# A fused DLRM tower on Trainium2: two weight loads and a gather wait change places in SyncE's program

## Chip, cores, metric

One core of one Trainium2 chip. The metric is the device time of one execution in microseconds. The kernel before has a median of 537.44 us over three runs (534.53 to 537.46).

## The reference, cut to what matters

A batch of 512 samples looks up one row of 1024 numbers in each of eight tables. Two of the eight fields pass a two-layer "not" net (Wn1 with relu, Wn2 with tanh). Then pairs of fields are fused by "and" nets (Wa1, Wa2) and one "or" net (Wo1, Wo2), the results and the unprocessed fields are averaged, and three top layers follow. Everything is float32.

```python
x_not = jnp.take(field_vectors, not_idx, axis=1)
t = jnp.tanh(jax.nn.relu(x_not @ Wn1 + bn1) @ Wn2 + bn2)
iv = field_vectors.at[:, not_idx, :].set(t)
...
and_out = pair_fuse(and_pairs, Wa1, ba1, Wa2, ba2)
or_out = pair_fuse(or_pairs, Wo1, bo1, Wo2, bo2)
...
z = sum_res / count
h = jnp.maximum(jnp.concatenate([z, dense_ctx], axis=1) @ W_top1 + b_top1, 0.0)
h = jnp.maximum(h @ W_top2 + b_top2, 0.0)
y = h @ W_top3
```

## The kernel before

**Layout.** XR holds float32 activations in eight buffers, features on the partitions, batch along the free axis. WR holds seven slots of raw weights, 128 x 1024 float32 (512 KB) each, called pieces; piece n covers two output tiles of one quadrant of a weight matrix. Each piece is split for TensorE into a high and a low part: ScalarE copies WR to WO with rounding (split_w, L631), VectorE subtracts (L846) and raises w_lo. Activations are split in the same way into XO (L718 and L852 for the first field; L660 and L924 later). A product group is the twelve matmuls of 128 x 512 of one output tile (four k tiles, times high x high, high x low, low x high; L1117); each raises the semaphore quarter by one. Two groups use one piece.

**The big layers.** The matrices Wn1, Wn2 and Wa1 are multiplied by a scheme of seven products over 2 x 2 blocks, which needs sums of activation blocks (operand_sum, L986) and of weight quadrants. For Wn1 ("stage 0") the products come in the order P1, P2, Q5, Q6, Q7, P4, Q3. P1 uses the quadrant B11 (pieces 0 and 1, in WR slots 0 and 1) on the first "not" field, P2 the quadrant below it (pieces 2 and 3, in slots 4 and 5) on the same field. Q5 needs B11 + B12: once P1 has been fed, the two pieces of B12 are loaded into slots 2 and 3 (L465) and VectorE adds them to slots 0 and 1 (L866, raising t1_sum). ScalarE later copies these sums to slots 2 and 3 (L782), where GpSimd's accumulating DMA (add_quadrant, L526) adds a third quadrant for Q6.

**The start.** GpSimd gathers the rows of the first not field in four indirect DMAs (L496, semaphores x0_in[0..3]) and of the second in four more (L500, x1_in[0..3]). TensorE transposes them, in between the first product groups (L1144 for the first field, L1193 for the second), ScalarE copies the transposed banks out to XR (x0_keep at L724, raising x0_raw; x1_keep at L729, raising x1_raw), and P1's groups run on half the batch at a time, as rows come in.

**Who decides the order.** Each engine has its own program, written out by hand, and works it in order; between engines there are only semaphores. SyncE issues nearly all weight loads: load(n) (L448) puts piece n in its slot and raises raw_in of that slot. At the start it issues load(0) and load(1), then waits for x0_in[1] and issues load(2), waits for x1_in[3] (L460) and issues load(3), P2's second piece. Then come the two loads of B12, each behind a wait for x0_raw, 5 for the first and 6 for the second (x0_done(1, h) is 5 + h: the third and fourth of the four copies at L724 that stand in a row there). Then load(8) and all others follow, behind waits on quarter and w_lo.

**Readers near the change.** VectorE's program has, in this order: the four low parts of the first field's second half (L852), the two L866 (each waits for its raw_in), split_w(2), whose w_lo = 3 P2's first group waits for, and split_w(3), whose w_lo = 4 P2's third group waits for. ScalarE splits piece 2 (L631), copies the second field's banks (L729), evacuates P1 (L689), splits piece 3 (L631), makes the two copies L782, and copies the last two banks of the second field (L729), which P2's third and fourth groups need freed. TensorE transposes the second field's second half before P2's first group and again between its first and second (turn_second_field(1, ...), L1193).

Of the kernel before, what the change touches and what calls it, by code (L numbers as in the profile page):

```python
# [22 lines left out]
BT = B // P  # L23
# [111 lines left out]
def raw_slot(n):  # L135
    if n >= 2 * OZ:
        return (n - 2 * OZ) % 7
    if n in R_PIECES:
        return R_SLOT + R_PIECES.index(n) % 3
    s, half = stage_of(n // 2), half_of(n // 2)  # L140
    if s == 0 and product_of(n // 2) in (Q6, P4):
        return 2 + n % 2
    return 2 * (half if s == 2 else s) + n % 2
# [15 lines left out]
def x_done(e, kk):  # L159

    return x0_done(1, 2 * e + kk) if e < 2 else 8 + 2 * (e - 2 - sum(e >= i for i in KEPT_X)) + kk + 1


def x0_done(h, pair):


    return 4 * h + pair + 1
# [63 lines left out]
def dlrm_tower(nc, table, ints, weights, cols, consts, identity, dense_t, w_dense, out, zero_row):  # L231
    table_quarters = table.rearrange("v (q c) -> (v q) c", q=Q)

    with ExitStack() as ctx:
# [3 lines left out]
        def sem(name):  # L238
            return ctx.enter_context(nc.semaphore(name))
# [80 lines left out]
        x1_in = [sem(f"x1_in{b}") for b in range(BT)]  # L320
# [97 lines left out]
        def block_rows(n):  # L418

            e, h = n // 2, n % 2  # L420
            if e < OZ:
                kh, mh = LOADED[product_of(e)]
                return 8 * matrix_of(e) + 4 * mh + 2 * h, k_half(e, kh)
            if 2 * n < FIRST[Z]:
                i = n - 2 * OZ
                return 8 * (4 + i // 8) + 2 * (i % 4), i // 4 % 2
            i = n - FIRST[Z] // 2
            if 2 * n < FIRST[TOP]:
                matrix, kh, mh = Z_PARTS[i // 2]
                return 8 * matrix + 4 * mh + 2 * (i % 2), kh  # L430
            return 8 * KT + 2 * (i % 2), i // 2 - len(Z_PARTS)

        def quadrant_rows(block, kh):
            return weights[block:block + 2, :, 512 * kh:512 * (kh + 1)].rearrange("m p c -> p m c")

        def raw_piece(slot):
            return WR[:, slot, :].rearrange("p (m c) -> p m c", m=2)
# [4 lines left out]
        @block.sync  # L442
        def _(sp):
            sp.dma_start(int_in, ints).then_inc(ints_in, 16)

            def load(n):
                slot = raw_slot(n)
                sp.dma_start(raw_piece(slot), quadrant_rows(*block_rows(n))).then_inc(raw_in[slot], 16)  # L448

            def load_after(n, split):  # L450

                sp.wait_ge(w_lo, split + 1)
                load(n)

            load(0)
            load(1)

            sp.wait_ge(x0_in[1], 16)
            load(2)
            sp.wait_ge(x1_in[BT - 1], 16)  # L460
            load(3)

            for h in range(2):
                sp.wait_ge(x0_raw, x0_done(1, h))
                sp.dma_start(raw_piece(2 + h), quadrant_rows(4 + 2 * h, 0)).then_inc(raw_in[2 + h], 16)  # L465
            sp.wait_ge(quarter, 4)
            load(8)
            for n, split in ((9, 2), (12, 3), (13, 8), (16, 9), (14, 10), (15, 11), (17, 12), (20, 13), (28, 14),
# [4 lines left out]
                load_after(n, split)  # L473
            for n in range(63, PIECES - 1):
                load_after(n, n - 7)
            sp.wait_ge(x_lo, x_done(Z - 1, 1))
            sp.wait_ge(dense_zero, 1)
            for i in range(3):
                sp.dma_start(dense_raw[DG * i:DG * i + DENSE, 0:B], dense_t).then_inc(dense_in, 16)
                sp.dma_start(dense_raw[DG * i:DG * i + DENSE, B:], w_dense).then_inc(dense_in, 16)  # L480
            last = PIECES - 1
            sp.wait_ge(w_lo, last - 6)
            sp.dma_start(WR[:, raw_slot(last), :],
                         weights[DENSE_K:DENSE_K + 1, :, :].rearrange("o p c -> p (o c)"))\
                .then_inc(raw_in[raw_slot(last)], 16)

            sp.wait_ge(y_ready, 1)
            sp.dma_start(out.rearrange("b o -> o b"), y_sb).then_inc(out_done, 16)
            sp.wait_ge(out_done, 16)
# [861 lines left out]
```

## Time and profile before

| | us |
|---|---|
| median of three runs | 537.44 |
| lowest and highest run | 534.53, 537.46 |
| the profiled execution's own time | 535.43 |
| span of its trace, first to last instruction | 533.6 |
| TensorE busy, products | 527.0 (99%) |
| VectorE, ScalarE, GpSimd busy | 360.9, 250.4, 241.6 |

Times of rows count from the start of the span. PE is TensorE's products, PEld its weight loads (they run beside the products), DVE VectorE, ACT ScalarE, POOL GpSimd, SP SyncE; a q behind the name means the engine's instruction queue, where DMAs are issued. L12 is line 12 of the kernel. "<-" in brackets says what ended the idle time ahead of an instruction; it is inferred from semaphore events. The granted clock of TensorE was 1.00, its full speed, in the whole span of the products. The execution's own time is 1.8 us more than its span, which leaves out what lies before the first and behind the last instruction.

### The profile page before, as it was taken

What the parts mean: (1) busy time and instruction counts of PE and PEld (TensorE: products, weight loads), DVE (VectorE), ACT (ScalarE), POOL (GpSimd) and SP (SyncE); (2) the same over time, 40 slices, a digit from 0 to 9 for tenths busy, and PEclk for the clock granted to TensorE, in tenths of its full rate; (3) what the DMA queues carried; (4) which work ended last, traced back from release to release, by engine and by line L of the source; (5) the groups of instructions that cost most, each with busy time, mean ns of one, the idle gap of its engine ahead of it and who ended that gap; (6) DMA issues with size and microseconds to landing.
All of it is one profiled execution on the core that took longest, in us unless ns stands there. A gap on an engine that the chain in (4) does not pass through costs nothing.

```text
span 533.6 us, 6218 instructions
## 1 busy us (share of the span) xinstructions
PE 527.0 (99%) x2385; PEld 437.0 (82%) x2385; DVE 360.9 (68%) x366; ACT 250.4 (47%) x305; POOL 241.6 (45%) x202
## 2 busy tenths in 40 slices
PE   8989999999999999999999999999999999999998
PEld 6978888888888888888888888888888888888885
DVE  5358899999785786787549788533332883678732
ACT  3675575747366453634446545232244433134343
POOL 5038876589856503551563258888566000000000
PEclk9999999999999999999999999999999999999999
DMA  7779665755895655678395358245999223241000
GB/s 261 248 198 215 127 214 165 180 152 130 198 216 157 120 119 152 110 130 160 95 269 161 117 150 273 79 120 114 242 262 232 97 89 110 83 123 48 0 0 1
DMA packets 39536, 78.95 MB, mean 148 GB/s; under 512 B 7281, under 2 KB 7537, under 8 KB 39506
## 3 DMA queue, kind: packets, MB, share of 16 engines
q0 software_dynamic: 19552, 40.93, 34.7%
q1 hardware_dynamic: 19522, 37.51, 23.0%
q8 instruction: 19, 0.31, 0.2%
q10 hardware_dynamic: 432, 0.11, 0.1%
q14 instruction: 11, 0.09, 0.0%
HBM read 86.90 MB, written 0.00 MB: 163 GB/s over the span
## 4 chain that ended last, share of the span: by engine, by line
PE 93%; DMA 3%; POOL 1%; DVE 1%; issue 1%; ACT 0%; SPq 0%
PE PS L1117 92%; DMA XR<-table,rows 2%; DMA WR<-weights 1%; PE PS L1288 1%; POOL XR L496 1%; POOL XR L500 1%; DMA XR<-ints 0%; PE PS L1295 0%; DVE WR L866 0%; DVE WO L846 0%; PE PS L1125 0%; PE PS L1193 0%; ACT XR L789 0%; ACT XR L792 0%; SPq L465 0%
## 5 line engine op out<-in xcount | busy, mean ns | idle before, releaser
L1117 PE MATMUL PS<-XO,WO 128*128 128x512 f32 (+1 forms) x2256 | 503.4, 385 | 1.7 <-DVE WO L846 1.7
L1117 PEld LDWEIGHTS PS<-XO,WO 128*128 128x128 f32 x2256 | 417.1, 188 | 86.2 <-DVE WO L846 1.9
L631 ACT ACTIVATE WO<-WR 128x1024 fp32r<-128x1024 f32 x93 | 98.6, 1060 | 238.8 <-PE PS L1117 233.7
L846 DVE TENSOR_TENSOR WO<-WR,WO 128x1024 fp32r<-128x1024 f32 x93 | 113.9, 1225 | 125.7 <-ACT WO L631 122.0
L510 POOL DMA_INDIRECT XR<-table,rows x96 | 124.5, 1297 | 94.6 <-PE PS L1117 61.3
L660 ACT ACTIVATE XO<-XR 128x1024 fp32r<-128x1024 f32 (+1 forms) x76 | 79.2, 1045 | 2.5 <-DVE XR L986 2.5
L924 DVE TENSOR_TENSOR XO<-XR,XO 128x1024 fp32r<-128x1024 f32 x60 | 73.0, 1218 | 0.7 <-ACT XO L660 0.7
L599 POOL DMA_INDIRECT XR<-table,rows_rest x32 | 53.8, 1681 | 15.4 <-issue 9.8
L526 POOL DMA_DIRECT2D WR<-weights x30 | 38.2, 1542 | 45.9 <-DVE WO L846 20.6
L937 DVE STREAM_TRANSPOSE XR<-XR 128x1024 f32<-128x1024 f32 x24 | 51.6, 2150 | 0.0
L986 DVE TENSOR_TENSOR XR<-XR 128x1024 f32<-128x1024 f32 (+1 forms) x32 | 38.7, 1218 | 1.8 <-ACT XR L729 1.8
L665 ACT ACTIVATE XR<-XR,col 128x512 f32<-128x512 f32 x36 | 25.5, 714 | 8.5 <-DVE XR L1009 8.4
L689 ACT ACTIVATE XR<-PS 128x512 f32<-128x512 f32 x40 | 23.5, 588 | 3.6 <-PE PS L1117 3.6
L921 DVE SCALAR_TENSOR_TENSOR XO<-XR,XO 128x1024 fp32r<-128x1024 f32 x16 | 19.4, 1219 | 0.8 <-ACT XO L660 0.8
L613 POOL DMA_DIRECT2D XR<-XR x32 | 17.1, 545 | 5.0 <-DMA XR<-table,rows_rest 5.0
L1009 DVE TENSOR_TENSOR XR<-PS,XR 128x512 f32<-128x512 f32 x20 | 13.6, 685 | 3.1 <-issue 1.8
L1149 PE MATMUL PS<-XO 128*128 128x512 f32 x33 | 10.4, 467 | 1.5 <-DVE XO L811 1.5
L1023 DVE SCALAR_TENSOR_TENSOR XR<-PS,inv,XR 128x512 f32<-128x512 f32 x8 | 6.0, 750 | 7.1 <-PE PS L1117 7.1
L852 DVE TENSOR_TENSOR XO<-PS,XO 128x512 fp32r<-128x512 f32 x8 | 5.2, 687 | 7.5 <-ACT XO L718 6.2
L1149 PEld LDWEIGHTS PS<-XO 128*128 128x128 f32 x33 | 7.3, 231 | 3.0 <-DVE XO L811 1.5
L697 ACT ACTIVATE XR<-PS,col 128x512 f32<-128x512 f32 x12 | 8.1, 676 | 1.7 <-PE PS L1117 1.6
L1009 DVE TENSOR_TENSOR XR<-XR,PS 128x512 f32<-128x512 f32 x12 | 8.2, 686 | 0.7 <-PE PS L1117 0.7
(74 smaller groups left out, 119.5 us busy)
## 6 DMA issues: line engine op xcount, KB each, us to landing
WR<-weights SPq DMA_DIRECT2D x71, 512.0 KB
WR<-weights POOLq DMA_DIRECT2D x30, 512.0 KB, 6.9
XR<-XR POOLq DMA_DIRECT2D x32, 64.0 KB, 5.2
XR<-table,rows POOLq DMA_INDIRECT x104, 8.3
XR<-table,rows_rest POOLq DMA_INDIRECT x32
XR<-dense_t SPq DMA_DIRECT2D x3, 32.0 KB, 3.8
XR<-w_dense SPq DMA_DIRECT2D x3, 32.0 KB, 3.6
XR<-ints SPq DMA_DIRECT2D x1, 84.0 KB, 2.1
```

The source lines that it names most:

```text
L510: pool.indirect_dma_start(to[:, QC * g:QC * (g + 1)], None, table_quarters, bass.IndirectOffsetOnAxis(ap=rows[:, slot - 1, 8 * h + g:8 * h ...
L526: pool.dma_start(raw_piece(slot), quadrant_rows(8 * matrix_of(e) + 4 * mh + 2 * h, kh), accum_op=ALU.add).then_inc(w_sum[slot], 16)
L599: pool.indirect_dma_start(rest_tile(b), None, table, bass.IndirectOffsetOnAxis(ap=rows_rest[:, b, f:f + 1], axis=0), compute_op=ALU.add if ...
L631: nc.scalar.activation(WO[:, n % 2, 0, :], WR[:, slot, :], ACT.Copy).then_inc(w_hi, 1)
L660: nc.scalar.activation(XO[:, s1:s1 + 2, 0, :], source(e, kk, regs), ACT.Copy, scale=scale)\
L665: nc.scalar.activation(place(s, which, m), place(s, which, m), FUNC[s], bias=bias_of(s, which, m)).then_inc(c_out[which], 1)
L689: nc.scalar.activation(place(s, KEPT[s][j], m), PS[:, bank, :], ACT.Copy).then_inc(kept, 1)
L846: V_.tensor_tensor(WO[:, n % 2, 1, :], WR[:, raw_slot(n), :], WO[:, n % 2, 0, :].bitcast(FP32), ALU.subtract).then_inc(w_lo, 1)
L924: V_.tensor_tensor(lo, source(e, kk, regs), hi, ALU.subtract).then_inc(x_lo, 1)
L937: V_.transpose(XR[:, SLOT_BUF[slot], :, b:b + 128].rearrange("p k (g b) -> p g k b", b=32), staging(slot, h)[:, 1024 * (i % 2):1024 * (i % ...
L986: V_.tensor_tensor(out, one, two, ALU.subtract).then_inc(sums, 1)
L1117: mm = nc.tensor.matmul(PS[:, bank, cols], WO_t[:, slot, ws, i, k, :], XO[:, x0 + k, xs, cols], start=first and k == 0 and n == 0, stop=la ...
```

## The change

In SyncE's program the wait for x1_in[3], the last gather of the second not field, and load(3) move from ahead of the two loads of Wn1's B12 to behind them. No instruction is added or taken away, and no other engine's program changes.

```diff
             sp.wait_ge(x0_in[1], 16)
             load(2)
-            sp.wait_ge(x1_in[BT - 1], 16)
-            load(3)
 
             for h in range(2):
                 sp.wait_ge(x0_raw, x0_done(1, h))
                 sp.dma_start(raw_piece(2 + h), quadrant_rows(4 + 2 * h, 0)).then_inc(raw_in[2 + h], 16)
+            sp.wait_ge(x1_in[BT - 1], 16)
+            load(3)
             sp.wait_ge(quarter, 4)
             load(8)
```

## Rows read from the trace of the kernel before

**Rows 1.** The page: busy time by engine, and the last-ending chain by engine.
```profile
PE 527.0 (99%) x2385; PEld 437.0 (82%) x2385; DVE 360.9 (68%) x366; ACT 250.4 (47%) x305; POOL 241.6 (45%) x202
...
PE 93%; DMA 3%; POOL 1%; DVE 1%; issue 1%; ACT 0%; SPq 0%
```

**Rows 2.** Waits of TensorE, whole trace: us in total, times, longest.
```profile
PE PS L1117 <- DVE WO L846: 1.7, 1, 1.7
PE PS L1149 <- DVE XO L811: 1.5, 1, 1.5
PE PS L1144 <- issue: 1.1, 1, 1.1
```

**Rows 3.** The chain of waits, 13 to 36 us: start, us, what.
```profile
13.29 9.01 DMA XR<-table,rows
...
22.32 0.37 SPq L448
...
22.73 0.47 SPq L465
...
23.25 6.45 DMA WR<-weights
...
32.13 3.03 PE PS L1117 x12
```

**Rows 4.** Timeline of VectorE, 28 to 34 us: start, us, engine, line.
```profile
28.45 2.49 DVE L866 TENSOR_TENSOR WR<-WR 128x1024 f32<-128x1024 f32 x2 [3.54 <-DMA WR<-weights]
30.86 1.22 DVE L846 TENSOR_TENSOR WO<-WR,WO 128x1024 fp32r<-128x1024 f32 x1
32.56 1.23 DVE L846 TENSOR_TENSOR WO<-WR,WO 128x1024 fp32r<-128x1024 f32 x1 [0.48 <-ACT WO L631]
```

**Rows 5.** The chain of waits from 36 us on.
```profile
36.05 478.75 PE PS L1117 x2112
...
515.03 2.74 PE PS L1117 x12
```

**Rows 6.** Timeline of ScalarE, the L724 copies from 18.75 us.
```profile
18.75 2.08 ACT L724 ACTIVATE XR<-PS 128x512 f32<-128x512 f32 x4
```

**Rows 7.** Timeline of SyncE, load(0) with load(1), and load(2).
```profile
1.22 0.93 SPq L448 DMA_DIRECT2D WR<-weights  x2
...
11.86 0.37 SPq L448 DMA_DIRECT2D WR<-weights  x1
```

**Rows 8.** Windows of 0.5 us; last columns granted clock, DMA share, GB/s.
```profile
20.50:21.00 0.50, 0.50 (x6) 0.50 (x5) 0.00 (x0) 0.33 (x1) 0.00 (x0) 1.00 0.04 12
...
22.50:23.00 0.50, 0.50 (x7) 0.50 (x6) 0.00 (x0) 0.00 (x0) 0.00 (x0) 1.00 0.00 0
```

**Rows 9.** Timeline of ScalarE, the split of piece 0.
```profile
6.05 1.06 ACT L631 ACTIVATE WO<-WR 128x1024 fp32r<-128x1024 f32 x1 [3.13 <-DMA WR<-weights]
```

**Rows 10.** GpSimd's weight DMAs (L526) issued by 62 us.
```profile
DMA to landing us min/median/max: 6.2/7.4/8.6
```

**Rows 11.** Timeline of TensorE's products, then of its weight loads, 29 to 33 us.
```profile
29.35 1.06 PE L1193 MATMUL PS<-ident,XR 128*128 128x128 f32 x8
...
32.13 2.60 PEld L1117 LDWEIGHTS PS<-XO,WO 128*128 128x128 f32 x12 [1.90 <-DVE WO L846]
```

**Rows 12.** Timeline of ScalarE, piece 3's split and the last L729 pair.
```profile
31.46 1.07 ACT L631 ACTIVATE WO<-WR 128x1024 fp32r<-128x1024 f32 x1
...
35.64 1.09 ACT L729 ACTIVATE XR<-PS 128x512 f32<-128x512 f32 x2 [0.73 <-PE PS L1193]
```

**Rows 13.** Timeline of GpSimd, and its waits from 54 to 76 us.
```profile
34.27 2.55 POOL L526 DMA_DIRECT2D WR<-weights  x2 [20.05 <-ACT WR L782]
...
58.36 2.60 POOL L526 DMA_DIRECT2D WR<-weights  x2
...
POOL XR L510 <- PE PS L1117: 1.1, 2, 0.8
```

**Rows 14.** Line L526, whole trace; and ScalarE's split at 71.54 us.
```profile
DMA to landing us min/median/max: 6.2/6.9/11.8
...
71.54 1.06 ACT L631 ACTIVATE WO<-WR 128x1024 fp32r<-128x1024 f32 x1 [1.24 <-PE PS L1117]
```

## Prediction

> **What bounds the kernel now.** I read the page first. TensorE is busy for nearly the whole span and the last-ending chain is TensorE's own [rows 1], so a change pays only by what it takes out of TensorE's idle time or out of a chain that holds TensorE up. Next come the waits of TensorE: the largest of the whole trace is one of 1.7 us, on VectorE's L846, the weight split; the others, of 1.5 and 1.1 us, are at the very start [rows 2]. Then the chain of waits shows where the 1.7 us come from. Read backwards from the stall: the first product group of P2 begins at 32.13; before it VectorE's split L846, directly behind L866, its additions of the B12 pieces to the B11 pieces [rows 4]; before it a weight transfer of 6.45 us; before it the issues of L465, directly behind the issue of load(3) at 22.32; and before that the last gather of the second field, landing at 22.30 [rows 3]. So SyncE held the two B12 loads back until gather rows had come that those loads don't use. From 36.05 on the chain is one piece of TensorE's products, 478.75 us long and without a gap, followed by the tail [rows 5]. Whatever is won ahead of 36.05 therefore arrives at the end, unless a new wait opens in that piece.
>
> **What moves.** The change puts L465's two waits and two issues ahead of the wait for x1_in[3] and of load(3). Nothing is added or removed: the same three transfers of 512 KB, in the order B12 piece 0, B12 piece 1, P2's second piece.
>
> *When the B12 loads are issued.* Their own waits ask for x0_raw at 5 and 6, the third and fourth of ScalarE's four L724 copies. The four fill 2.08 us from 18.75, so the last is over at 20.83 and, at 2.08 / 4 = 0.5 us a copy, the third at 20.3 [rows 6]. SyncE has been free since its load(2) at 11.86 [rows 7]. So the issues start at 20.35 and, 0.47 us of issuing and the second wait later, at 20.88, where they now start at 22.73 and 23.20 [rows 3]: 2.4 and 2.3 us sooner.
>
> *When they land.* In this trace the first piece released L866 at 28.45 [rows 4], 5.7 us from its issue, and the second at 29.69 [rows 3], 6.5 us from its issue, both while three loads shared the engines. (L866's second addition would have started at 29.67 anyway, so that the 29.69 may hide a slightly earlier landing.) The DMA engines are nearly empty from 20.5 to 23.0: five slices of half a microsecond with a share of 0.06 at most, the first at 0.04 and the last at 0.00 [rows 8]. The moved loads fall into that hole and have no load(3) ahead of them. I take the measured times unchanged, the cautious side: 20.35 + 5.7 = 26.1 and 20.88 + 6.5 = 27.4. The bounds: as quick as the kernel's first weight load, issued at 1.22 and split by ScalarE at 6.05, 4.8 us [rows 7, 9], it would be 25.2 and 25.7; as slow as the slowest of GpSimd's weight DMAs in the first 60 us, 8.6 us [rows 10], it would be 29.0 and 29.5.
>
> *What VectorE makes of it.* It has nothing else to do before L866: 3.54 us idle ahead of it. Two additions of 1.24 and the split of 1.22 follow [rows 4]. From 27.4: second addition until 28.6, split until 29.8. Its other operand, ScalarE's high part of piece 2, was made by then: the split now runs directly behind the additions, without waiting for ScalarE [rows 4]. With the quick bound the additions are through by 27.7 and the split by 28.9; with the slow one it is 29.5 + 1.24 + 1.2 = 31.9.
>
> *What TensorE makes of it.* The transposes ahead of P2 run from 29.35 for 1.06 us, so TensorE is free at 30.41 [rows 11]. P2 needs the split at that time. 29.8 leaves 0.6 us of cover, the quick bound 1.5; the slow bound would leave a stall of 1.5, of 1.7 now. So the stall of 32.13 - 30.41 = 1.7 us goes. The first group of P2 took 3.03 us from its cold start while an ordinary group of the same twelve products takes 2.74 [rows 3, 5]; the weight load of its first product (idle 1.90 where the products idled 1.71, [rows 11]) would now run under the last transposes. That is up to 0.3 more. I take 0.2 of it: gain 1.7 + 0.2 = **1.9 us**, with bounds 2.0 and, by the slow landing, 31.95 - 30.41 = 1.5 less, 0.2; a landing like the gather's 9.0 us [rows 3] would even cost 0.2.
>
> *What is late next.* P2's second group follows at 30.4 + 2.75 + 0.9 of transposes (it starts at 36.05 now, [rows 5]), so at about 34.1, its third at 36.9. That third needs two things. One is the split of piece 3, now over at 33.79 [rows 4]: its release by ScalarE at 31.46 stands directly behind other ScalarE work and doesn't move, cover 3.1 us [rows 12]. The other is the bank freed by the first L729 of the pair now at 35.64. ScalarE waited 0.73 us for TensorE there; with the transposes early it starts when the two L782 copies end, at 34.91, and the bank is free at 35.5: cover 1.4 [rows 12]. GpSimd's first accumulating load hangs on those L782, in ScalarE's order, so it stays at 34.27 [rows 13] while TensorE comes 1.9 us sooner. GpSimd then issues without a real pause until 58.36, waits 0.30 and 0.83 for TensorE on its way to 74.44 and lands its weight additions 6.9 us (median) after their issue. The one at 58.36 is then there by 65.3, and ScalarE splits it at 71.54, or 69.6 after the change, cover 4 us [rows 13, 14]. Everything later is released by splits and product counts, so it moves with TensorE.
>
> *load(3).* Its wait still ends at 22.30, so its issue stays at about 22.3 [rows 3]. All three transfers together had landed by 29.69; with two of them started earlier the third should be no later than that, 1.8 us ahead of its reader at 31.46 [rows 3, 12]. Cost nothing; if the cover goes, see the third rival.
>
> Of what the DMA engines do with two queues the trace shows this: the last gather's landing came at 22.30, 1.8 us after the engines had all but emptied at 20.5 [rows 3, 8]. The new issues fall between the two. The Trainium skill ("DMA: Bandwidth & Descriptors", section "Queues, rings and completion order") says that an engine serves its queue rows in turn and that the write which raises a semaphore lands only behind every earlier write of that engine, in whichever queue. By it the early B12 data could hold up that landing, and load(3) with it; no row here separates the two queues. The sum by the rows is 1.9; by the rule it would be rival 3's.
>
> **The sum.** Against the profiled execution, 535.43 us with a span of 533.6, the forecast is 533.5 and a span of 531.7. The median shown is 2.0 above that execution, and the runs lie at 534.53, 537.44 and 537.46: a scatter wider than the effect. Median minus 1.9 is 535.5; the mean of all four executions, 536.2, minus 1.9 is 534.3. I forecast **535.0**, between the two.
>
> **Rivals.** *(1) Landing eats it (12 in 100).* The two B12 loads take the 8 to 9 us of the slow bound and P2 starts at 31.9. For it: the second landing was only bounded by the trace. Against it: the empty slices. Gain 0 to 0.5: 537.2 by the median, 535.2 by the profile.
> *(2) Given back later (8 in 100).* The stall goes and TensorE waits later on a weight addition or a gather half that GpSimd issues at fixed times up to 74 us. For it: GpSimd starts at the same 34.27. Against: 4 us of cover, and no TensorE wait in 478.75 us. If one piece came 5 us late, 1 us of the 1.9 would be lost: 536.5 by the median, 534.5 by the profile.
> *(3) Slower (4 in 100).* The early loads delay the landing of the second field's last gather, load(3) is issued late behind it, and ScalarE, which works in order, stands at piece 3's split with two more copies (L782) and the bank-freeing L729 queued behind it. From that split at 31.46 to the free bank at 35.5 it is 4.0 us [rows 12]. P2's third group starts at 36.05 + 2.74 = 38.8 now, at 36.9 in the forecast: load(3) may land until 32.9 at no cost, eats into the gain from there, and makes the kernel slower from 34.8 on, 12.5 us behind its present issue. If x1_in[3] came only with the first B12 piece, at 26.1, and load(3) took the longest landing of a weight DMA in the trace, 11.8 us [rows 14], that would be 37.9, 3.1 us slower: 540.5 by the median, 538.5 by the profile. With a landing of 6.9 us it would be 33.0, and the gain stays whole. The Trainium skill's rule quoted above would be its mechanism. Against it: the gathers' data is through by 20.5, and it takes both mishaps.
> *The forecast* has 76 in 100.
>
> **Range.** 532.4 to 537.3: below, the lowest run shown minus 2.1; above, the median with a gain of nearly nothing, which takes in rivals 1 and 2. A measurement of this kernel tells about 1% from no change, 5.4 us; no case reaches that, so "within 1%" takes 95, faster 3 and slower 2 in 100, for the scatter between the runs.
>
> **What would show it.** In the changed profile: two L465 issues at 20.4 and 20.9 and load(3) at 22.3; the three L866/L846 of VectorE starting at 25 to 26.1 and over before 29.9; no TensorE wait on L846, P2's first group at 30.4; later no TensorE wait at all; span near 531.7. Wrong if L866 still starts after 27.5 (rival 1), if a TensorE wait appears between 34 and 75 us (rival 2), or if ScalarE's L631 of piece 3 waits for a DMA (rival 3).

## The result, and the profile after

| | before | after |
|---|---|---|
| median of 12 executions, us | 537.36 | 533.41 |
| lowest and highest, us | 534.39, 539.0 | 532.68, 534.79 |
| profiled execution, its span, us | 535.43, 533.6 | 533.45, 531.6 |

The ratio is 0.9936, with a 95% interval from 0.9919 to 0.9954: the change makes the kernel 0.6% faster, clear of no change though under 1%. The time lies in the stated range, 1.6 us below the forecast. The profiled execution gained 2.0 us, as forecast (1.9), but the median gained 3.9 us. The second difference between the two columns is the scatter: 4.6 us before, 2.1 us after. Both go back to the same stall, as the runs below show.

First the steps that were forecast. SyncE's timeline of the changed kernel, the two B12 loads (L463 now) and load(3) as the first of its row:

```profile
19.83 1.25 SPq L463 DMA_DIRECT2D WR<-weights  x2
...
22.40 0.37 SPq L448 DMA_DIRECT2D WR<-weights  x1
```

The loads go out at 19.8 and, by the end of the row, at 20.6 us; the forecast had 20.35 and 20.88, from a profile in which TensorE and ScalarE were 0.5 us later at that point. load(3) hasn't moved (22.32 in [rows 3]). VectorE's timeline after:

```profile
24.96 1.23 DVE L866 TENSOR_TENSOR WR<-WR 128x1024 f32<-128x1024 f32 x1 [0.58 <-DMA WR<-weights]
26.38 1.23 DVE L866 TENSOR_TENSOR WR<-WR 128x1024 f32<-128x1024 f32 x1 [0.19 <-DMA WR<-weights]
27.52 1.22 DVE L846 TENSOR_TENSOR WO<-WR,WO 128x1024 fp32r<-128x1024 f32 x1
32.02 1.23 DVE L846 TENSOR_TENSOR WO<-WR,WO 128x1024 fp32r<-128x1024 f32 x1 [3.28 <-ACT WO L631]
```

Both additions still end an idle time that a weight DMA ended, but at 24.96 and 26.38 where [rows 4] have 28.45 for the first, and P2's split is over at 28.74. TensorE, products only, needs it at the end of its transposes:

```profile
28.81 1.06 PE L1193 MATMUL PS<-ident,XR 128*128 128x128 f32 x8
29.63 3.01 PE L1117 MATMUL PS<-XO,WO 128*128 128x512 f32 x12
```

The brackets with a wait are gone: no idle time stands ahead of P2's first group, and the cover (how long before TensorE's need the split is over) is 1.1 us. The list of what TensorE's products waited for holds only the wait at the start of the program:

```profile
PE PS L1149 <- DVE XO L811: 1.5, 1, 1.5
```

The chain of waits of the changed kernel stays on TensorE from its start, with one exception:

```profile
28.98 0.90 PE PS L1193 x8
29.88 2.77 PE PS L1117 x12
32.64 0.88 PE PS L1193 x8
33.52 43.95 PE PS L1117 x192
...
77.56 1.07 ACT WO L631
78.63 0.02 issue
78.65 1.24 DVE WO L846
79.89 0.04 issue
79.93 432.91 PE PS L1117 x1908
```

The long stretch of products began at 36.05 in [rows 5] and begins at 33.52 here, 2.5 us sooner. 1.7 of that is the stall, 0.3 its cold first group (the first after a pause, 3.03 us in [rows 3], 2.77 here), and 0.5 an earlier start of this execution. At 79.93 TensorE's weight loads had to wait once for a split, and 0.6 us went back; the waits from 56 to 80 us have it as

```profile
PEld PS L1117 <- DVE WO L846: 0.6, 1, 0.6
```

That wait is followed up below.

### The profile page after: what moved, and what is told of

The parts are those of the page before. It is cut to its first block, busy times and chain, and to the rows that moved or that the text cites. A ratio compares the mean times of both kernels' runs of the same rounds, so it can differ in the third digit from the quotient of the medians.

```text
span 531.6 us, 6218 instructions
## 1 busy us (share of the span) xinstructions
PE 527.7 (99%) x2385; PEld 437.8 (82%) x2385; DVE 360.8 (68%) x366; ACT 249.8 (47%) x305; POOL 248.6 (47%) x202
## 4 chain that ended last, share of the span: by engine, by line
PE 99%; ACT 0%; DVE 0%; issue 0%; ACTq 0%
PE PS L1117 94%; PE PS L1149 2%; PE PS L1288 1%; PE PS L1193 1%; PE PS L1144 1%; PE PS L1295 0%; DVE WO L846 0%; ACT WO L631 0%; PE PS L1125 0%; ACT XR L789 0%; ACT XR L792 0%; DVE XO L811 0%; ACTq L630 0%
## 5 line engine op out<-in xcount | busy, mean ns | idle before, releaser
L510 POOL DMA_INDIRECT XR<-table,rows x96 | 130.8, 1363 | 85.8 <-PE PS L1117 55.1
L526 POOL DMA_DIRECT2D WR<-weights x30 | 38.2, 1571 | 45.9 <-DVE WO L846 21.7
L937 DVE STREAM_TRANSPOSE XR<-XR 128x1024 f32<-128x1024 f32 x24 | 51.6, 2150 | 0.2 <-DMA XR<-table,rows 0.2
L1033 DVE STREAM_TRANSPOSE XR<-XR 128x1024 f32<-128x1024 f32 x4 | 8.5, 2116 | 0.0
```

What stands on the lines that cost most here:

```text
L510: pool.indirect_dma_start(to[:, QC * g:QC * (g + 1)], None, table_quarters, bass.IndirectOffsetOnAxis(ap=rows[:, slot - 1, 8 * h + g:8 * h ...
L526: pool.dma_start(raw_piece(slot), quadrant_rows(8 * matrix_of(e) + 4 * mh + 2 * h, kh), accum_op=ALU.add).then_inc(w_sum[slot], 16)
L937: V_.transpose(XR[:, SLOT_BUF[slot], :, b:b + 128].rearrange("p k (g b) -> p g k b", b=32), staging(slot, h)[:, 1024 * (i % 2):1024 * (i % ...
```

## The experiments

**Why is the median's gain larger than the profile's?** Two theories. A: the stall ahead of P2 differs from execution to execution, and the profiled one was short. B: it is always near 1.7 us and the rest comes from elsewhere. The kernel before was profiled twice more, and two variants took the change apart into its order and its wait.

> The unchanged kernel before, looked at once more. Theory A (TensorE's stall ahead of P2 differs from one execution to the next with the landing of the second field's last gather and of the three loads; the profiled execution was one with a small stall): the stall in this profile is anything from 1.5 to 6 us, and span minus stall is 531.9 us within 0.6. Theory B (the stall is always near 1.7 us and the rest of the median's gain comes from elsewhere): stall 1.7 within 0.4 us, whatever the span.

> The kernel before once more, for the same question. Theory A: a stall that differs from the other two profiles of this kernel by more than 0.5 us, span minus stall 531.9 within 0.6. Theory B: stall 1.7 within 0.4 us.

Measured: 535.24 and 536.84 us, spans of 533.4 and 535.0. TensorE's timeline of b1_before_again:

```profile
28.88 1.06 PE L1193 MATMUL PS<-ident,XR 128*128 128x128 f32 x8
31.97 3.04 PE L1117 MATMUL PS<-XO,WO 128*128 128x512 f32 x12 [2.02 <-DVE WO L846]
```

and of b2_before_again:

```profile
28.33 1.06 PE L1193 MATMUL PS<-ident,XR 128*128 128x128 f32 x8
32.00 4.56 PE L1117 MATMUL PS<-XO,WO 128*128 128x512 f32 x12 [2.60 <-DVE WO L846]
```

In both P2 begins at the same time, 31.97 and 32.00: in both the chain of waits runs from B12's transfer through VectorE to P2. In the second TensorE merely arrived 0.55 us earlier and waited longer, 2.6 us for 2.0. And then its first group took 4.56 us for 3.04. The windows of b2_before_again show why; the third column from the right is the granted clock:

```profile
32.50:33.00 0.50, 0.50 (x3) 0.40 (x3) 0.50 (x2) 0.50 (x2) 0.00 (x0) 1.00 0.00 0
33.00:33.50 0.50, 0.50 (x3) 0.37 (x2) 0.50 (x2) 0.50 (x1) 0.25 (x1) 0.63 0.42 98
33.50:34.00 0.50, 0.50 (x3) 0.40 (x2) 0.50 (x1) 0.39 (x1) 0.50 (x1) 0.50 0.75 238
...
36.50:37.00 0.50, 0.50 (x7) 0.50 (x6) 0.00 (x0) 0.00 (x0) 0.50 (x1) 0.96 0.75 201
```

After the stall the clock stands at 0.50 (1.2 GHz) in place of 1.00 (2.4 GHz) from 33.1 until 36.5 us; windows of 0.1 us have 0.65 at 33.1 and 0.79 at 36.5. From P2's start to the long stretch of products that costs 1.6 us: from 32.00 to 37.49 here, from 31.97 to 35.89 in b1_before_again. The Trainium skill ("TensorE: Matmul & The Clock Gate", section "Part 1: The HAM clock gate (the "warmup" mystery)") has the clock at one of two levels, by how busy the engine was; the trace agrees, with 1.00 and 0.50 in these windows and the fall behind a stall.

Theory A was half right. Span minus stall is 531.4 in b1 and 532.4 in b2, 531.9 in the first profile: inside the stated band, but with the 1 us between them unexplained by the stall alone. The missing part is the clock: 1.6 us less the 0.55 that TensorE was early. Call that theory D. It can be read off every execution, since each has its mean granted clock beside its time. Executions of the kernel before, in three sets of runs timed together (one of 3057.78 us is left out):

```
set             clock 1.000: count, lowest to highest    below 1.000: count, lowest to highest
b1, e1, e2, b2   2   535.22 to 535.41                     9   536.59 to 538.33
e5, e3, e4, a1   6   534.57 to 535.88                    19   536.71 to 539.19
a2, e6           2   535.51 to 535.84                     8   536.79 to 539.74
```

Of 46 executions 36 lost clock, and no time of the one kind lies among the other. Four of the 36 have a mean of 0.994 where the others have 0.997, so they lost about twice as much, and they are the slowest, 538.84 to 539.74. None of them was profiled; where they lose it the second time isn't known. The profile on which the forecast rested was one of the rarer kind.

**The order alone.** Before, the wait for the gather stood ahead of load(3) and of the B12 loads. e1 leaves it there and changes only the order of the loads.

```diff
             sp.wait_ge(x1_in[BT - 1], 16)
-            load(3)
 
             for h in range(2):
...
+            load(3)
             sp.wait_ge(quarter, 4)
```

> SyncE waits for the second field's last gather first, then issues the two B12 loads, then load(3): the new order with the old wait. Theory A (the wait is what costs, the order is worth one transfer's time): B12 issued right behind the gather's landing, second landing 6 us later instead of 7.4, a stall of about 1.3 us less than before: median 1.3 us below the kernel before, 2 us or more above the changed kernel, and the scatter of before stays. Rival C (the order is what counts): median within 0.5 us of the changed kernel. Theory B: 536.0 to 536.5.

Measured: 533.82 us (533.33 to 534.91), ratio 0.9943 (0.9925 to 0.9960), clock 1.00 in all six. The chain of waits of e1_wait_first:

```profile
22.78 5.29 DMA WR<-weights
...
30.52 3.03 PE PS L1117 x12
```

and its list of TensorE's waits:

```profile
PE PS L1117 <- DVE WO L846: 1.0, 1, 1.0
```

The transfer's part was right: the second piece lands at 28.07, 1.6 us before the 29.69 of [rows 3], and the stall is 1.0 us. The time was not: a gain of 1.3 us and the old scatter were expected, and 3.25 us (537.07 against 533.82) and a scatter of 1.6 were measured. With a stall of 1.0 us in the profile no execution lost clock.

**The wait alone.** e2 keeps the old order; load(3) waits for the same copy as the first B12 load and no longer for the gather.

```diff
-            sp.wait_ge(x1_in[BT - 1], 16)
+            sp.wait_ge(x0_raw, x0_done(1, 0))
             load(3)
             for h in range(2):
...
```

> The old order, load(3), then the two B12 loads, but load(3) waits only for the same copy as the first B12 load and no longer for the gather. Theory A: issues at about 20.4, 20.8 and 21.2, second B12 landing by 28, TensorE's wait ahead of P2 under 0.4 us: median within 0.4 us of the changed kernel, small scatter. Rival C: a stall of 1 us or more and a median at least 1 us above the changed kernel.

Measured: 534.04 us (533.24 to 534.25), ratio 0.9940 (0.9923 to 0.9956), clock 1.00 in all. The chain of waits of e2_old_order:

```profile
20.99 7.23 DMA WR<-weights
...
30.66 3.07 PE PS L1117 x12
```

The transfer took 7.23 us with load(3) ahead of it, against 5.8 in the changed kernel, where the same load went out at much the same time (20.6) with only the first B12 load ahead of it. TensorE's wait was 0.92 us where I expected under 0.4; the clock was kept all the same. So either half is enough to win most of the median's gain (3.3 and 3.0 us), and the halves don't add: in each the stall is near 1 us and the clock is kept. The rival that only the order counts had e1 right (within 0.5 us of the changed kernel's 533.41) and e2 wrong: 0.6 us above it, where 1 us or more was expected. What the clock alone is worth is tested next.

**Fill the stall and leave it.** If theory D holds, work that does nothing but keep TensorE busy must win what the clock costs.

```diff
+                    if (e, m) == (1, 0):
+                        bank_ready(0)
+                        for _ in range(6):
+                            nc.tensor.matmul(PS[:, BANK_B, :], XO[:, 4, 0, 0:P], XO[:, 4, 0, :], start=True, stop=True,
+                                             skip_group_check=True)
                     if t % 2 == 0:
                         pe.wait_ge(w_lo, t // 2 + 1)
```

> The kernel before, with six idle products of 128 x 512 on TensorE (their sums are overwritten by P2's first group) between the transposes and the wait for P2's first split. They fill about 1.4 us of the stall and move nothing: the end of the stall is still set by the B12 loads. Theory D (in most executions of before the stall of 2 to 3 us is followed by a stretch at half the granted clock, as in b2_before_again, where a group took 4.56 us instead of 3.03): no loss of clock, every execution near the fast ones of before, median 535.4 with a scatter under 2 us, about 1.7 us below the kernel before. Theory A without the clock (the length of the stall alone differs): the median stays within 0.5 us of before's 537.1.

Measured: 535.73 us (534.95 to 538.02) against 537.17, ratio 0.9981 (0.9965 to 0.9998); 11 of 12 executions at clock 1.00, the twelfth, 538.02, below it. TensorE's timeline of e5_filled_stall:

```profile
29.94 1.64 PE L1254 MATMUL PS<-XO 128*128 128x512 f32 x6
32.11 3.05 PE L1117 MATMUL PS<-XO,WO 128*128 128x512 f32 x12 [0.53 <-DVE WO L846]
```

P2 begins no sooner than before, at 32.11, and the median is 1.4 us lower. (Six products filled 1.64 us, 2.2 with the wait behind them.) This separates the two terms. About 1.4 us of the median's loss was clock; the interval of the ratio allows 0.1 to 1.9 us, but the counts are plain, 1 of 12 executions with lost clock against 19 of 25 beside them. The rest is the stall with its cold first group: the variant e4 below, which is as fast as the changed kernel and was timed in the same set, has 532.83, 2.9 us less than e5, and in the profiles its span is 2.7 us shorter (530.9 against 533.6). The scatter was 3.1 us rather than under 2, because of the one execution that lost clock.

**Later still.**

```diff
-                sp.wait_ge(x0_raw, x0_done(1, h))
+                sp.wait_ge(x0_raw, x0_done(1, 2 + h))
```

> The kernel before, with the B12 loads behind the seventh and eighth copy of the first field instead of the fifth and sixth: issues at about 24.5 and 25.0 us, 1.8 us later than before, with load(3) already under way. Theory D: the stall grows by about 1.5 us to 3.5 to 4 us, the clock is lost in every execution, about 1.7 us more: median 538.5 to 539.5, granted clock mean below 1.00 in all. Theory A without the clock: 1.5 us above before's median with no change of the clock.

Measured: 537.92 us (536.95 to 538.52), ratio 1.0020 (1.0003 to 1.0037), clock below 1.00 in all ten. The chain of waits of e3_late_b12:

```profile
24.97 4.67 DMA WR<-weights
...
32.08 4.60 PE PS L1117 x12
```

Half missed. The loads were issued 1.7 us later, at 24.38 and 24.97, and the last landed at 29.64, no later than in [rows 3]: the piece's own transfer shrank from 6.45 to 4.67 us. That in the old order the B12 loads stood behind load(3)'s data, so that their issue had slack, fits this, but no row separates the loads' data. The stall (2.3 us) did not grow as expected. That here every execution lost clock, and not only four in five, explains part of the small loss: the mean of the kernel before is 537.0 us over all 25 executions and 537.5 over the 19 that lost clock, e3's is 537.8. The last 0.3 us stay open.

**As early as can be.** e4 is the changed kernel without the B12 loads' own waits.

```diff
-                sp.wait_ge(x0_raw, x0_done(1, h))
```

> The changed kernel without the waits of the B12 loads: they are issued directly behind load(2), at about 11.5 us, among the gathers. Theory D with contention: 1 MB more on engines that are full until 20 us, so the first field's last gathers and the second field's come 1 to 3 us later, TensorE waits for rows at its transposes ahead of P1's second half (17 to 22 us), and the kernel is 0.5 to 3 us slower than the changed one, with less clock if the wait is over 2 us. The rival (early is harmless, since the additions are read late): within 0.3 us of the changed kernel.

Measured: 532.83 us (532.67 to 533.34), ratio 0.9927 (0.9900 to 0.9955), clock 1.00 in all. The gathers do land later, and it costs nothing. Landings of the second field's four gathers (minimum, median, maximum) were, in the changed kernel,

```profile
DMA to landing us min/median/max: 7.8/7.9/8.5
```

and in e4_unpaced

```profile
DMA to landing us min/median/max: 7.7/9.9/10.7
...
24.04 0.37 SPq L448 DMA_DIRECT2D WR<-weights  x1
```

The gathers land up to 2 us later and load(3) is issued at 24.04 in place of 22.40, but the last of them lands at 24.0, and TensorE transposes the rows of the last two gathers only from 28.6 us on; ScalarE splits load(3)'s piece at 30.7. I expected a loss of 0.5 to 3 us; the delay was there and its cover held. To see whether the early version is in fact better, both were timed side by side.

> The changed kernel on the same chip and in the same rounds as e6_unpaced_again: is the version without the B12 loads' own waits any faster? If those waits still cost something, the changed kernel is 0.3 us or more slower than e6; if everything ahead of P2 is covered in both, they agree within 0.3 us, with no clock lost in any execution of either (532.7 to 534.8). In the profile: no TensorE wait on L846 ahead of P2; ScalarE late by 1 us or more somewhere from 71 to 78 us, as in after and a1_after_again, if that belongs to the earlier TensorE.

> e4_unpaced once more, timed beside the changed kernel. Both covered: same time within 0.3 us. Rival (pacing costs): 0.3 us or more faster than the changed kernel. Theory D holds in both: granted clock 1.00 in every execution.

Measured: 532.77 us (532.44 to 532.99) and 532.69 us (532.50 to 532.97), ratios to before 0.9911 (0.9886 to 0.9936) and 0.9909 (0.9884 to 0.9934), clock 1.00 in all. They are the same. Ahead of P2 everything is covered in the changed kernel, and nothing tried here beats it by an amount that was measured. Here the changed kernel stands 5.0 us below the median of the kernel before (537.80), 4.8 by the ratio, where the first measurement had 3.9 and 3.4.

**The wait at 79 us.** In the first profile of the changed kernel TensorE waited for piece 11's split. ScalarE's timeline there:

```profile
69.02 1.06 ACT L631 ACTIVATE WO<-WR 128x1024 fp32r<-128x1024 f32 x1 [1.24 <-PE PS L1117]
...
73.18 0.60 ACT L689 ACTIVATE XR<-PS 128x512 f32<-128x512 f32 x1 [1.67 <-remote]
...
77.56 1.06 ACT L631 ACTIVATE WO<-WR 128x1024 fp32r<-128x1024 f32 x1 [3.17 <-PE PS L1117]
```

Splits stand 5.44 us apart otherwise, two groups; this one comes 8.5 us behind the one before it.

> The changed kernel once more. Is the small wait of TensorE at 79 us (0.56 us of weight loads idle, behind ScalarE's split of piece 11, 3.17 us late) part of the change? If GpSimd's fixed start makes it (rival 2 of the prediction), it stands here again, 0.3 us or more; if it is one late landing, it is absent and the span is 531.0 to 531.3.

Measured: 532.67 us, span 530.9. ScalarE is late again, but less, and TensorE doesn't wait:

```profile
75.82 1.06 ACT L631 ACTIVATE WO<-WR 128x1024 fp32r<-128x1024 f32 x1 [3.13 <-remote]
```

In a2_after_timed and e6_unpaced_again the same split comes on time, in a2_after_timed at

```profile
74.02 1.06 ACT L631 ACTIVATE WO<-WR 128x1024 fp32r<-128x1024 f32 x1 [1.57 <-PE PS L1117]
```

So this is no fixed part of the change: the lateness stood in two of three profiles of the changed kernel and cost 0.6 us in one. What makes ScalarE late stays open. The profile names TensorE in one case and "remote" in the other, and TensorE had long been done. In the program this split also waits for GpSimd's addition to piece 11, and the two late profiles show no landing for it (8.1 and 9.9 us for its pair in a2_after_timed), so a late landing isn't excluded. But the copy at 73.18 above waits for a product count alone and was 1.5 us late too. No run was made to find out.

## Why the prediction was right, and where not

- *The bound and the place.* Right: the 1.7 us wait was the only one to be had, and removing it moved the long stretch of products, which came through to the end.
- *Issue times.* Right within 0.5 us (19.8 against 20.35, with the whole start that much earlier).
- *Landing.* Right in its cautious form. Landings took 5.1 and 5.8 us where 5.7 and 6.5 were assumed, so the cover was 1.1 us and not 0.6. The order mattered by itself: 5.29 us in e1 against the 6.45 of [rows 3] with load(3) ahead, issued at the same time.
- *TensorE's gain in one execution.* Span 531.6, forecast 531.7, and the stall went as forecast, with 0.26 us of the cold group where 0.2 was put. That the two spans agree so well is luck: two things of 0.5 us each, an earlier start and the wait at 79 us, happened to cancel. The other two profiles of the changed kernel have spans of 530.9 and 530.6.
- *The median.* The measured 533.4 lies in the range, but a range from 532.4 to 537.3 takes in nearly every gain from 0 to 5 us, so that says little for the sum. The step that was mis-sized is "Median minus 1.9 is 535.5", and the choice of 535.0 between it and the mean. I took the 2 us between the profiled execution and the median as scatter that has nothing to do with the change, and placed the forecast between the two. It has to do with it. In 36 of 46 executions of the kernel before clock was lost; in the one of them that was profiled the same stall was 2.6 us long, and the clock stood at half for 3.4 us behind it. The term that was left out is the clock, 1.4 us of the median by e5 and 1.6 us in one execution by b2 against b1; and the stall itself, 1.7 us in the profile of the forecast, was 2.0 and 2.6 in the other two. Clock (1.4) and stall with cold group (2.7 to 2.9) add up to 4.1 to 4.3 us, between the 3.4 to 3.9 of the first measurement and the 4.8 to 5.0 of the later one.
- *Rival 1,* the landing eats the gain: no. *Rival 2,* given back later: once, 0.6 us, in one of three profiles, on the second piece of the pair that GpSimd issued at 58.36 in the forecast's profile, but not shown to be for the rival's reason. The cover of 4 us was too large: GpSimd issues that pair at 59.38, 59.18 and 58.95 in the three profiles of the changed kernel, not sooner, and in a2_after_timed its first piece landed 8.1 us later, 1.5 us before its split at 68.58. *Rival 3:* its first half does occur when B12's data and the gathers share the engines (e4), at 2 us, inside the cover; the second half does not. In the changed kernel not even the first half occurs: the last gather landed 8.5, 8.9 and 8.1 us after its issue in the three profiles, against 9.0, 8.7 and 8.5 in those of the kernel before. The Trainium skill ("DMA: Bandwidth & Descriptors", section "Queues, rings and completion order"), as the prediction quotes it, has the write that raises a semaphore land behind every earlier write of its engine in whichever queue. e4's gathers agree in direction, 10.7 us against 8.5, but no run here tells this from plain sharing of full engines.

## What to carry to other kernels

Price a stall of TensorE with what comes after it: look at the duration of the first group behind it and at the granted clock, in more than one execution. When the executions of a kernel lie in two bands and their mean clocks do too, the profile of one band doesn't give the median. And a stall whose end is set by a transfer gets longer when everything ahead of it goes well: P2 began at 32.0 whether TensorE arrived early or late. Here a shorter stall was worth more than its own microseconds, because with about 1 us of stall no execution lost clock.

## What the runs showed of the hardware that was not expected

TensorE's clock survived stalls of 1.7 and 2.0 us and fell after stalls of 2.3 and 2.6 us (products' idle time in four profiles), to 0.50 for 3.4 us both times. In b2_before_again the fall came 1.1 us after the work had resumed; in e3_late_b12, where P2 begins at 32.08, it came just then (mean granted clock 0.58 from 32.0 to 32.5 us), and that is why the first group there took 4.60 us. In e1 and e2, with stalls of 1.0 and 0.9 us in their profiles, no execution of twelve lost clock. The runs show no sharp length: the stall is known only in the profiled executions, and with the stall filled to 0.53 us in its profile, e5 still lost clock in one of twelve.
